# A macaron block on one core: attention weights and values as half-precision pairs, and the values' last half behind the scores

## The reference, cut to what matters

```python
x = x + 0.5 * ffn(layernorm(x))        # gate = sigmoid(x @ gate_w + b), broadcast from the last token
x = x + attn(layernorm(x))
x = x + 0.5 * ffn(layernorm(x))
# attn, for a block of 128 queries and the 256 keys of the block before and its own:
sim  = where(keep, q @ k2.T / 128, 0)
attn = square(relu(sim))
out  = (attn @ v2) @ w_o.T
```

## Time and profile before

| | |
|---|---|
| time, median of 3 runs | 2074.18 us (2071.38 to 2074.87) |
| profiled execution | 2078.41 us, its span 2077.2 us |
| PE busy | 1988.2 us, 96% |
| VectorE busy | 1207.6 us, 58% |
| ScalarE busy | 679.7 us, 33% |
| float32 matmuls of the collects, L1203 | 114.3 us busy, 248 records |

### The profile page before, as it was taken

The page is one execution under the profiler, slowest core; times in us unless marked ns, Lnnn a source line. Parts: engine busy times, 40 slices in busy tenths (PEclk is TensorE's granted clock), DMA queues, the critical chain, the costliest instruction groups (busy, mean ns, idle before and its releaser), DMA issues.

```text
span 2077.2 us, 30589 instructions
## 1 busy us (share of the span) xinstructions
PE 1988.2 (96%) x12010; PEld 1048.1 (50%) x12010; DVE 1207.6 (58%) x2152; ACT 679.7 (33%) x947; POOL 162.0 (8%) x278
## 2 busy tenths in 40 slices
PE   8999988999899899999999999999999999999997
PEld 3334433344343457655566655566656564444443
DVE  2323676223444465567666655655556536888887
ACT  0478545213223322223333212121112213444443
POOL 0000000000000010011001000000000001111111
PEclk9999998999999999999999999999999999999999
DMA  9599986879899743359989999798998947555552
GB/s 364 201 350 412 379 309 233 335 261 379 323 399 389 280 136 102 102 175 314 325 290 331 319 317 296 279 365 300 297 305 281 348 171 193 152 152 153 153 154 78
DMA packets 275214, 555.78 MB, mean 268 GB/s; under 512 B 149040, under 2 KB 149248, under 8 KB 274688
## 3 DMA queue, kind: packets, MB, share of 16 engines
q1 hardware_dynamic: 275072, 553.83, 76.6%
HBM read 406.93 MB, written 113.26 MB: 250 GB/s over the span
## 4 chain that ended last, share of the span: by engine, by line
PE 43%; DMA 4%; DVE 4%; SPq 2%; ACT 1%; issue 1%; POOL 0%; ACTq 0%; DVEq 0%
PE product_banks L1068 38%; PE product_banks L1203 2%; PE thought_acc L1268 2%; DMA thought_units<-parts_scratch 2%; DMA arena<-in_x 1%; SPq L989 1%; SPq L851 1%; DVE thought_units L1851 1%; DVE bn_parts L1492 0%; DMA gate_arena<-arena 0%; DMA arena<-x_scratch 0%; ACT arena L1384 0%; DVE arena L1663 0%; DVE arena L1639 0%; ACT arena L1387 0%
## 5 line engine op out<-in xcount | busy, mean ns | idle before, releaser
L1068 PE MATMUL product_banks<-gate_arena,arena 128*128 128x512 f16 x1536 | 355.5, 387 | 0.0
L1068 PE MATMUL product_banks<-wide_a,thought_units 128*128 128x512 f16 x1536 | 331.7, 379 | 0.8 <-DVE arena L1703 0.8
L1068 PE MATMUL product_banks<-gate_arena,wide_a 128*128 128x256 f16 x2688 | 301.6, 273 | 2.2 <-DMA gate_arena<-arena 2.2
L1068 PE MATMUL product_banks<-wide_b,gate_arena 128*128 128x512 f16 x1344 | 297.5, 379 | 0.0
L1068 PEld LDWEIGHTS product_banks<-gate_arena,wide_a 128*128 128x128 f16 x2688 | 261.6, 98 | 49.2 <-issue 19.3
L1068 PEld LDWEIGHTS product_banks<-gate_arena,arena 128*128 128x128 f16 x1536 | 150.6, 100 | 197.3 <-issue 40.4
L1068 PEld LDWEIGHTS product_banks<-wide_a,thought_units 128*128 128x128 f16 x1536 | 150.2, 98 | 182.6 <-DVE arena L1703 1.6
L1068 PEld LDWEIGHTS product_banks<-wide_b,gate_arena 128*128 128x128 f16 x1344 | 129.3, 98 | 160.8 <-issue 12.2
L1492 DVE BATCH_NORM_STATS2 bn_parts<-arena 128x6 f32<-128x512 f32 x256 | 164.2, 683 | 4.2
L1915 POOL TENSOR_TENSOR token_stats<-stats,minus_half 128x1 f32<-128x1 f32 x96 | 63.7, 664 | 1001.5 <-DVE stats L1500 848.4
L1672 DVE SCALAR_TENSOR_TENSOR gate_arena<-product_banks,gate_arena 128x256 f16<-128x256 f32 x128 | 54.1, 422 | 148.2 <-ACT gate_arena L1399 146.0
(11 more groups left out here) (206 smaller groups left out, 2310.9 us busy)
## 6 DMA issues: line engine op xcount, KB each, us to landing
thought_units<-parts_scratch SPq DMA_DIRECT2D x272, 512.0 KB, 6.9
thought_units<-in_d_w SPq DMA_DIRECT2D x171, 512.0 KB, 7.5
arena<-in_x SPq DMA_DIRECT2D x64, 512.0 KB, 9.3
...
```

The lines of the kernel that those rows point to most:

```text
L1068: mm = pe.matmul(bank, left(i, k), right(j, k), start=(n == 0), stop=(n == 3 * KD - 1))
```

## The change

1. Weights and values become f16 pairs. The place of a float32 block (of `v` slots and of `key_weights`) holds its high and low part. A collect half is then 3 f16 matmuls for each block of keys where it was 1 float32 matmul.
2. For the values, ACT writes the high part (scaled by a constant) and a new piece `v_low` on DVE writes the low part; the bank is freed by DVE.
3. For the scores, DVE's second instruction writes the weight back into the PSUM bank, ACT copies it to f16 (`score_high`), and DVE subtracts (`score_low`), which frees the bank.
4. The sum of squares of `qk` is measured: ACT squares each row block of fold qk with a running sum, and a `norm` scale is made by another `scale_t`, `scale_a`, `scale_b` ahead of the first `prep_fetch`. The collect's add on DVE multiplies by `collect_scale`.
5. Order: of each group the last half of the values is computed behind the scores; that is tile 1, half 1 in groups 0 and 1 (it stood there before as well) and tile 0, half 1 in the others. In a collect, PE waits for the values of its own half only. What waited for the tokens' last reader (`score`) waits for these values (`tokens_read`). `time_of` counts a collect half 1.3 where it was 1.77 (not in the diff below).

```diff
@@ -398,14 +400,31 @@
+def plan_value(n, i, h):
+    return [("v", n, i, h, third) for third in range(3)] + [("v_low", n, i, h)]
...
     out = [("q", n, e) for e in range(KD)]
     if n:
...
-    for i in range(GROUP):
-        for h in range(HALVES):
-            out += [("v", n, i, h, third) for third in range(3)]
-    return out
+    order = [(i, h) for i in range(GROUP) for h in range(HALVES)]
+    last = order.pop(3 if n < B else 1)
+    def values(*order):
+        made = []
+        for i, h in order:
+            more = plan_value(n, i, h)
+            made = made[:-1] + [more[0], made[-1]] + more[1:] if made else more
+        return made
+    if n == 0:
+        return values(*order[:2]) + out + values(*order[2:]), plan_value(n, *last)
+    out += values(*order)
+    return out, plan_value(n, *last)
@@ -429,9 +448,10 @@
-def plan_attention(n):
+def plan_attention(n, values):
     out = [("x1_fetch", c) for c, (at, *_) in enumerate(COLLECTS) if at == n]
-    out += [("score", n, i, third) for i in (1, 0) for third in range(3)]
+    out += [("score", n, 1, third) for third in range(3)] + [("score_high", n, 1), ("score", n, 0, 0), ("score_low", n, 1)]
+    out += [("score", n, 0, third) for third in (1, 2)] + [("score_high", n, 0), values[0], ("score_low", n, 0)] + values[1:]
@@ -451,16 +471,8 @@
+        products, values = plan_products(n)
+        attention = plan_attention(n, values)
@@ -546,6 +558,7 @@
+    splits += [(kind, "norm") for kind in ("scale_t", "scale_a", "scale_b")] + [("rest",)]
@@ -723,9 +736,10 @@
-    value_slot = lambda u: v1_slot if u % GROUP else v0_slots[(u // GROUP) % 3]
...
+    value_parts = lambda u: in_parts(v1_slot if u % GROUP else v0_slots[(u // GROUP) % 3])
@@ -778,6 +793,10 @@
+    tokens_read = lambda n: BANK_AT[("v", n, 1, 1) if n < B else ("v", n, 0, 1)] + 1
@@ -979,7 +998,7 @@
-                    sp.wait_ge(product_full, BANK_AT[("score", n - 2, 0)] + 1)
+                    sp.wait_ge(product_full, tokens_read(n - 2))
@@ -1031,7 +1050,7 @@
-                    sp.wait_ge(product_full, BANK_AT[("v", GROUPS - 1, 1, 1)] + 1)
+                    sp.wait_ge(product_full, tokens_read(GROUPS - 1))
@@ -1196,13 +1215,13 @@
-                    for other in values:
-                        for half in range(HALVES):
-                            await_out(pe, ("v", other // GROUP, other % GROUP, half))
+                for other in values:
+                    await_out(pe, ("v", other // GROUP, other % GROUP, h))
                 for side, other in enumerate(values):
-                    mm = pe.matmul(bank_ap(key), weights_of(u)[:, side, :],
-                                   value_slot(other)[:, h * BANK:(h + 1) * BANK],
-                                   start=(side == 0), stop=(side == len(values) - 1))
+                    for n, (i, j) in enumerate(((0, 0), (0, 1), (1, 0))):
+                        mm = pe.matmul(bank_ap(key), weights_of(u, side)[:, i],
+                                       value_parts(other)[:, j, h * BANK:(h + 1) * BANK], start=(side == n == 0),
+                                       stop=(side == len(values) - 1 and n == PARTS - 1))
@@ -1311,6 +1330,13 @@
+                    if m == "qk":
+                        for h in range(HALVES):
+                            await_out(act, ("fold", m, d, h))
+                        act.activation(unit_at(FOR_SPLITS[0]), fold_slots[d % FOLD_RING], ACT.Square,
+                                       accum_out=scale_stat["norm"][:, d:d + 1]).then_inc(largest["norm"], 1)
+                        act.wait_ge(largest["norm"], d + 1)
@@ -1402,8 +1428,14 @@
-                act.activation(value_slot(n * GROUP + i)[:, h * BANK:(h + 1) * BANK], bank_ap(key), ACT.Copy,
-                               scale=inverse["vo"][:, :]).then_inc(out_of(key), 1)
+                act.activation(value_parts(n * GROUP + i)[:, 0, h * BANK:(h + 1) * BANK], bank_ap(key), ACT.Copy,
+                               scale=VALUE_SCALE).then_inc(value_high, 1)
+            elif kind == "score_high":
+                n, i = a
+                key = ("score", n, i)
+                act.wait_ge(weighed, SCORE_AT[n, i] + 1)
+                for at, (u, side, _) in enumerate(scores_of(n, i)):
+                    act.copy(weights_of(u, side)[:, 0], bank_ap(key)[:, at * P:(at + 1) * P]).then_inc(weights_high, 1)
@@ -1565,12 +1597,24 @@
-                dve.tensor_reduce(scale_stat[m][:, KD:KD + 1], scale_stat[m][:, 0:KD], AX_X, ALU.max).then_inc(
-                    top_found, 1)
+                dve.tensor_reduce(scale_stat[m][:, KD:KD + 1], scale_stat[m][:, 0:KD], AX_X,
+                                  ALU.add if m == "norm" else ALU.max).then_inc(top_found, 1)
...
+                if m == "norm":
...
+                    dve.tensor_scalar(exponent.bitcast(I32), top.bitcast(I32), 1, EXPONENT_BITS,
+                                      ALU.logical_shift_right, ALU.bitwise_and).then_inc(own.up(), 1)
+                    dve.wait_ge(own.sem, own.n)
+                    dve.tensor_scalar(scale.bitcast(I32), exponent.bitcast(I32), EXPONENT_BITS, None,
+                                      ALU.bitwise_xor).then_inc(own.up(), 1)
+                    dve.wait_ge(own.sem, own.n)
+                    dve.tensor_scalar(scale, scale, 2.0 ** -61, None, ALU.mult).then_inc(own.up(), 1)
+                    dve.tensor_scalar(inverse[m][:, :], exponent, 2.0 ** 60, None, ALU.mult).then_inc(scale_made, 1)
+                    continue
@@ -1598,8 +1642,16 @@
-                dve.tensor_scalar(score_scale[:, :], inverse["qk"][:, :], 1.0 / (QUERY_SCALE * TOKEN_SCALE * P),
...
+                dve.scalar_tensor_tensor(out=score_scale[:, :], in0=inverse["qk"][:, :],
+                                         scalar=1.0 / (QUERY_SCALE * TOKEN_SCALE * P),
+                                         in1=scale_stat["norm"][:, KD + 2:KD + 3], op0=ALU.mult,
+                                         op1=ALU.mult).then_inc(own.up(), 1)
...
+                dve.scalar_tensor_tensor(out=collect_scale[:, :], in0=inverse["vo"][:, :], scalar=1.0 / VALUE_SCALE,
+                                         in1=inverse["norm"][:, :], op0=ALU.mult, op1=ALU.mult).then_inc(own.up(), 1)
+                dve.wait_ge(own.sem, own.n)
+                dve.tensor_tensor(collect_scale[:, :], collect_scale[:, :], inverse["norm"][:, :],
+                                  ALU.mult).then_inc(own.up(), 1)
@@ -1682,17 +1734,36 @@
-                    to = weights_of(u)[:, side, :]
-                    dve.scalar_tensor_tensor(out=to, in0=bank_ap(key)[:, at * P:(at + 1) * P],
...
+                    masked, part = key_weights[:, weights_place(u), side, :], bank_ap(key)[:, at * P:(at + 1) * P]
+                    dve.scalar_tensor_tensor(out=masked, in0=part, scalar=score_scale[:, :], in1=keep[:, :],
+                                             op0=ALU.mult, op1=ALU.min).then_inc(own.up(), 1)
                     dve.wait_ge(own.sem, own.n)
-                    last = dve.scalar_tensor_tensor(out=to, in0=to, scalar=0.0, in1=to, op0=ALU.max, op1=ALU.mult)
+                    last = dve.scalar_tensor_tensor(out=part, in0=masked, scalar=0.0, in1=masked, op0=ALU.max,
+                                                    op1=ALU.mult)
                     if at < len(found) - 1:
                         last.then_inc(own.up(), 1)
+                    else:
+                        last.then_inc(weighed, 1)
...
+            elif kind == "score_low":
...
+                dve.wait_ge(weights_high, sum(len(scores_of(*at)) for at, m in SCORE_AT.items() if m <= SCORE_AT[n, i]))
+                for at, (u, side, _) in enumerate(found):
+                    low = dve.tensor_tensor(weights_of(u, side)[:, 1], bank_ap(key)[:, at * P:(at + 1) * P],
+                                            weights_of(u, side)[:, 0], ALU.subtract)
+                    if at < len(found) - 1:
+                        low.then_inc(own.up(), 1)
                         dve.wait_ge(own.sem, own.n)
                     else:
-                        last.then_inc(out_of(key), 1)
+                        low.then_inc(out_of(key), 1)
+            elif kind == "v_low":
+                n, i, h = a
+                key, parts = ("v", n, i, h), value_parts(n * GROUP + i)[:, :, h * BANK:(h + 1) * BANK]
+                dve.wait_ge(value_high, VALUE_AT[n, i, h] + 1)
+                dve.scalar_tensor_tensor(out=parts[:, 1], in0=bank_ap(key), scalar=VALUE_SCALE, in1=parts[:, 0],
+                                         op0=ALU.mult, op1=ALU.subtract).then_inc(out_of(key), 1)
@@ -1700,7 +1771,8 @@
-                dve.tensor_tensor(xs[:, cols], bank_ap(key), xs[:, cols], ALU.add).then_inc(out_of(key), 1)
+                dve.scalar_tensor_tensor(out=xs[:, cols], in0=bank_ap(key), scalar=collect_scale[:, :], in1=xs[:, cols],
+                                         op0=ALU.mult, op1=ALU.add).then_inc(out_of(key), 1)
```

31 lines of the change are left out of this document (14 added, 17 removed).

## The result

The changed kernel took 2071.12 us (median of 18 runs, 2064.85 to 2074.06), the kernel before 2076.84 on the same chip (18 runs, 2069.91 to 2082.49): ratio 0.997, 95% interval 0.996 to 0.998, some 6 us faster. The forecast was 25.6 us faster, with a range of 2038 to 2062 us. The direction was right, the size wrong by 20 us. The profiled execution has a span of 2068.8 us, 8.4 less than before.

The account below looks back on a forecast made before the run. PE, busy 1988 of 2077 us, was taken as the bound. Terms -29.3 - 5.6 - 1.7 + 3.3 + 1.2 + 3.5 + 3.0 gave -25.6 us: 2048.6 from the median of 2074.2, range 2038 to 2062.

Parts of the forecast that it names:

- Step 1: Attention's collects: 124 float32 products become 372 f16 matmuls, 109.7 us to 80.4, a gain of 29.3 us.
- Step 2: PE's waits before collects fall from 9.5 us to 3.9, a gain of 5.6, plus 1.7 us of clock.
- step 4: End of the attention: PE waits 3.4 us instead of 0.8 before the second gate; +3.3 us with lost clock.
- 1.7 us lost; that should go: Clock lost in one attention group after a wait before a collect; 1.7 us expected to be regained.
- Step 3: Attention: DVE gains 63 us of work, ACT 15; neither is full, so nothing is charged here.
- step 6: Attention's other waits, 12.7 us: 3 us more expected (0 to 12), from nearly full DMA engines and fuller DVE.
- Step 5: Norm scale before the attention: +1.2 us for ACT's squares, +3.5 for PE's wait of 3.1 and the new matmul.
- the 10 that the prediction named as a sign of being wrong: Attention: the forecast is wrong if waits for transfers grow beyond 10 us.
- The rival of the transfers: Attention: PE's savings turn into transfer waits, losing half of 27 us in groups 2 to 14; 2062 us, chance 0.13.
- the rivals: Nothing comes back (chance 0.12), transfers take it back (0.13), DVE's queue bounds PE (0.03), weights' loads show (0.02).
- 2.1 us a group: PE's saving in each of attention groups 3 to 13, as stated in the rival about transfers.

Follow-up runs that it names:

- run 12: Changed kernel with the third and fourth x3 fetches put behind the xs fetches in SP's order; ratio to the kernel before 0.9940.
- run 8: Changed kernel with low parts made for only 64 of each 512 and 16 of each 128 columns; ratio to the kernel before 0.9938.
- Runs 13 to 15 and 17: New order, ratios to before. Pairs, norm scale early, x3 behind xs: 0.9930 full, 0.9773 half-width fetches (13, 15). Float32: 0.9854 half-width (14), 0.9949 full with x3 behind xs (17).

## Why the prediction was wrong, step by step

The steps are compared within the two profiled executions, whose spans differ by 8.4 us where 25.6 were forecast.

- *Step 1, matmuls*: 27.1 us of busy time for 29.3. The products at the spacing of a stream cost what was said (30 in 6.47 us in run 12, 0.216 each); the rest is clock behind waits (12 records in 4.44 us in group 0, where a stream takes 2.75). Off by 2. The Trainium skill (FP8 and Floating Point Precision, TensorE Precision Notes) with its four passes for float32 gave 26.8. That is nearer by luck, for the 27.1 hold this lost clock, and a float32 product measured 0.885, above its 0.864. Its other figure, 131 ns a matmul in a stream of loads and matmuls (the Trainium skill, TensorE: Matmul & The Clock Gate, Back-to-back issue gap), is not borne out: the streams here show 216 to 224.
- *Step 2, waits before the collects*: the mechanism held, 3.3 us left without those of step 4, for 3.9. But "1.7 us lost; that should go" was wrong: the loss behind waits went from 3.0 to 6.3 us. Off by 5, less the 0.6.
- *Step 3, DVE and ACT*: DVE 637 us, ACT 240.5, for 646 and 247. That it was charged nothing was right for its busy time and not for its waits: PE's waits for DVE's part of the row grew by 4.3 us, and run 8 gained with DVE lighter. These are counted in step 6, where the prediction put them.
- *Step 4, end*: 3.6 us of waits for 3.4, and the second gate 1.5 longer for 0.7. Off by 1. The stretch at 1719.8 us lost another 1.2 of clock.
- *Step 5, norm scale*: the wait was as forecast, 2.96 us for 3.1 and the same in seven profiles. The stage is 7.0 us longer for 4.7 in this pair of profiles, and 4.6 on average over twelve. So the term was right; the 2 us are this execution's clock.
- *Step 6, what comes back*: this is the step that failed. It said 3 us (0 to 12). The stage's other waits went from 12.7 to 23.6 us: 10.9, of them some 6.4 for transfers and 4.3 for DVE's part of the row. Off by 8. The waits for transfers stand at 11.8 us, beyond the 10 that the prediction named as a sign of being wrong. Runs 13 to 15 and 17 show that it is no sum of small chances: with half-width fetches these waits grow by 4 us with the pairs, with full ones by 12. So some two thirds hang on the transfers, and the rest ends with DVE and stays open.

Together 18 us, for 17.2 between the profiles (steps 1 and 2 share a little of the clock); the rest of the 20 lies between this profiled execution (-8.4) and the medians (-5.7).

The rival of the transfers, at a chance of 0.13, named the mechanism of the larger part, but its 12 us of gain are twice the measured 6. None of the rivals had a cost for the clock behind the waits that come back.

The mistake behind step 6 was to read the transfers' share as a possible loss beside a sum made in PE's time. "PE waited little for transfers in that stage" was true and proved nothing. Waits tell what bounds a stage now, and not what will bound it 3% sooner. Another reading was at hand: 0.91 of the DMA engines over 570 us means that the same bytes need 519 us with no gap at all. The forecast's 2.1 us a group, some 19 us in these nine groups, asked for 519 of 551 us, 0.94. The changed kernel shows that share there, and from group 6's first q to group 14's it gained 8.8 us (495.1 to 486.3) where 17 were forecast. So the share warns, but it does not give the size of the loss; only the runs do. The share is the thing to read, not the bytes: the stretch at 979.8 us moved 419 GB/s at a share of 1.03, but that at 1164.8 only 328 at 0.99, and 1348 to 1358.5, under the transpose, 345 at 1.02. The Trainium skill (DMA: Bandwidth & Descriptors, Where 436 GB/s comes from) gives 435 GB/s as the ceiling of the ports. No stretch shown here is above it, but by that figure alone the 319 GB/s of the middle of the stage would look like a quarter free, where the engines' share is 0.94.
